# Weighted values of a head group: four key chunks in one TensorE burst instead of two bursts of two

## The reference

```python
# attention (x: 4 x 512 x 256, ctx: 4 x 512 x 256)
Q, K, V = heads(layernorm(x), Wq, bq), heads(ctx, Wk, bk), heads(ctx, Wv, bv)
scores = einsum('bhqd,bhkd->bhqk', Q, K) / sqrt(D) + adj
scores = where(mask == 0, -inf, scores)
out = einsum('bhqk,bhkd->bhqd', softmax(scores), V)     # the weighted values
x = x + tanh(g_xattn) * (out @ Wo.T + bo)
# experts (8, hidden 1024), one expert for each token by argmax of a softmax gate
x = x + tanh(g_ffn) * (relu(xn @ w1[e] + b1[e]) @ w2[e] + b2[e]) * gate_weight     # xn = layernorm(x)
```

## Time and profile before

| | us |
|---|---|
| median of 3 runs (lowest, highest) | 622.31 (622.23, 623.06) |
| profiled execution, its own time | 623.12 |
| its span | 621.3 |
| attention steps within the span | about 43 to 394 |
| PE busy in the span | 528.8 (85%) |
| DVE, ACT, POOL busy | 297.5, 303.9, 308.1 |
| line 821 on PE, 1024 records | 70.9 |

### The profile page before, as it was taken

The page is one execution under the profiler, slowest core; times in us unless marked ns, Lnnn a source line. Parts: engine busy times, 40 slices in busy tenths (PEclk is TensorE's granted clock), DMA queues, the critical chain, the costliest instruction groups (busy, mean ns, idle before and its releaser), DMA issues.

```text
span 621.3 us, 13413 instructions
## 1 busy us (share of the span) xinstructions
PE 528.8 (85%) x4008; PEld 401.0 (65%) x4009; DVE 297.5 (48%) x883; ACT 303.9 (49%) x674; POOL 308.1 (50%) x475
## 2 busy tenths in 40 slices
PE   4579999899999899999899988510989999999992
PEld 3247566566666566666566665310989999998882
DVE  2656677776678775678566876340011111111110
ACT  3536676556685556686566755200333333333320
POOL 6443485763584663584655537122344445445341
PEclk9879999999999899999899998955899999999997
DMA  8664139612149520149400181855455655555630
GB/s 294 213 215 138 64 103 210 136 68 70 40 139 198 102 69 2 60 133 194 92 2 2 51 271 45 288 108 138 113 184 181 204 191 205 195 190 185 186 93 1
DMA packets 62649, 83.43 MB, mean 134 GB/s; under 512 B 8920, under 2 KB 52008, under 8 KB 62472
## 3 DMA queue, kind: packets, MB, share of 16 engines
q1 hardware_dynamic: 58504, 74.53, 43.2%
q0 software_dynamic: 4096, 8.29, 4.6%
HBM read 69.54 MB, written 14.18 MB: 135 GB/s over the span
## 4 chain that ended last, share of the span: by engine, by line
PE 24%; DMA 16%; issue 9%; POOL 6%; DVE 5%; ACT 2%; POOLq 1%; DVEq 0%; SPq 0%; ACTq 0%
DMA out_y<-cT,sidx 13%; PE bank L809 6%; PE bank L821 5%; PE bank L799 3%; POOL rows L623 3%; PE bank L906 2%; PE bank L896 2%; DVE prob L1218 2%; DMA slot_d<-pair,posi 2%; PE bank L702 1%; ACT pt L986 1%; PE bank L783 1%; PE bank L737 1%; DMA rows<-xn_d,gidx 1%; PE bank L764 1%
## 5 line engine op out<-in xcount | busy, mean ns | idle before, releaser
L1218 DVE CUSTOM_DVE_ANT_0 prob<-bank,adjm 128x512 f32<-128x512 f32 x256 | 172.7, 688 | 95.5 <-issue 63.0
L571 POOL TENSOR_SCALAR prob<-prob,negmax 128x512 f32<-128x512 f32 x192 | 134.3, 704 | 143.4 <-DVE negmax L1218 135.4
L986 ACT ACTIVATE pt<-bank 128x512 f32<-128x512 f32 x256 | 150.9, 595 | 100.1 <-PE bank L809 94.4
L809 PE MATMUL bank<-ident,prob 128*128 128x128 f32 x1024 | 156.7, 276 | 7.3 <-POOL prob L571 3.4
L809 PEld LDWEIGHTS bank<-ident,prob 128*128 128x128 f32 x1024 | 126.7, 142 | 47.0 <-POOL prob L571 13.4
L1051 ACT ACTIVATE adjm<-bank,colsm 128x128 f32<-128x128 f32 x184 | 52.6, 368 | 113.9 <-PE bank L896 113.9
L799 PE MATMUL bank<-w2s 128*128 128x512 bf16 x256 | 99.4, 390 | 6.2 <-DMA w2s<-part_d 5.5
L1337 DVE TENSOR_TENSOR cT<-bank,maski 128x256 f32<-128x256 f32 x23 | 9.8, 424 | 172.1 <-PE bank L906 172.1
L896 PEld LDWEIGHTS bank<-xT,pt 128*128 128x128 f32 x736 | 88.3, 197 | 2.2 <-ACT xT L1042 1.0
L896 PE MATMUL bank<-xT,pt 128*128 128x128 f32 x736 | 88.6, 280 | 0.6 <-ACT xT L1042 0.6
L906 PE MATMUL bank<-w2s,adjm 128*128 x368 | 83.4, 380 | 0.0
(11 more groups left out here) (141 smaller groups left out, 502.3 us busy)
## 6 DMA issues: line engine op xcount, KB each, us to landing
pt<-in_L_ffn_w SPq DMA_DIRECT2D x23, 1024.0 KB
w2s<-part_d SPq DMA_DIRECT2D x48, 256.0 KB
w2s<-in_L_ffn_w SPq DMA_DIRECT2D x8, 1024.0 KB, 10.6
part_d<-parts SPq DMA_DIRECT2D x16, 384.0 KB, 2.6
maski<-in_mask_Bx1xSxS_ik SPq DMA_DIRECT2D x4, 1024.0 KB, 6.2
w2s<-part_d SPq DMA_DIRECT2D x32, 128.0 KB, 3.0
xres<-in_x SPq DMA_DIRECT2D x18, 128.0 KB
x_d<-rows SPq DMA_DIRECT2D x18, 128.0 KB, 2.5
```

The costliest lines, as they stand in the source:

```text
L571: po.tensor_scalar(prob[:, m], prob[:, m], -1.0, negmax[:, m:m + 1], ALU.mult, ALU.add).then_inc(s_shpool, 1)
L809: mm = pe.transpose(tr_bank[n % NTB][:, c * P:(c + 1) * P], prob[:, n % TILES % NB, c * P:(c + 1) * P], ident[:])
L986: act.activation(pt[:, g % 2, :, j, q2 * P:(q2 + 1) * P], tr_bank[c % NTB][:].rearrange("p (c q) -> p c q", c=QT), ACT.Exp).then_inc(s_cac ...
L1218: ve.tensor_tensor_reduce(out=prob[:, m % NB], in0=sc_bank[m % NS][:], in1=adjm[:, qt], scale=-1.0, scalar=BIG, op0=ALU.add, op1=ALU.min, ...
```

## The change

The test that picks the steps now picks every eighth step alone, and all four chunks run there, in step 13 + 8g. Step 15 + 8g has no weighted values any more. Nothing else changes: the same matmuls, the same semaphores, the same work on DVE, ACT, POOL and SyncE. The wait ahead of chunk 0 stays where it was, and the count that tells ACT that the group is done (`s_pv`) is given two steps earlier in the order.

```diff
-                if n >= LP + TPG and (n - LP) % TPG in (0, 2):
-                    g, c = divmod(n - LP - TPG, TPG)
-                    if g == 0 and c == 0:
+                if n >= LP + TPG and (n - LP) % TPG == 0:
+                    g = (n - LP - TPG) // TPG
+                    if g == 0:
                         pe.wait_ge(s_v, b * 2 + 2)
-                    weigh(b, g, c)
-                    weigh(b, g, c + 1)
+                    for c in range(QT):
+                        weigh(b, g, c)
```

## The result

| | before, same series | after |
|---|---|---|
| median (lowest to highest), 20 executions each, us | 623.59 (620.31 to 629.65) | 632.1 (625.88 to 636.22) |
| ratio, 95% interval | | 1.0132 (1.0106 to 1.0159) |
| profiled execution, own time and span, us | 623.12, 621.3 | 633.5, 631.7 |

The forecast was 624.6 with 620.3 to 627.5. The sign is right, the size is not: +8.2 us (6.6 to 9.9) against +2.3.

What follows compares the result with a forecast made beforehand. PE's order was taken to set the pace in the attention steps, PE being busy 85% of the span. Group gains and losses of +0.8 us plus +1.5 for clock falls gave +2.3, a median of 624.6 us, range 620.3 to 627.5.

Steps and rivals of the forecast that it cites:

- What joining saves: Each of 31 joins of two bursts saves 0.24 us of switching on PE, 7.4 us if PE waited for nobody.
- Steps 37 and 45 in batches 0 to 2, and 45 in batch 3: Joins there lose: +0.37 us through ACT's chain to `gate`, +0.86 through DVE's chain to `rank`.
- Batch 3: Last batch, where ACT has no next-batch work: groups of 13 to 37 gain 0.24 us each; whole batch -0.19.
- Group of step 61: `gate` of step 65 hangs on transposes of 64, behind both old bursts, so the join gains: -0.24 us.
- the group of 69: Both bursts lie inside POOL's `rstd` chain in batches 0 and 1: 0; batch 2 has no such work: -0.24 us.
- The cover term: Gains and losses of all groups over four batches sum to +0.8 us, bounds -0.7 to +2.8.
- The clock term: Emptier wait before `rank` drops PE's clock at two of four places: +1.5 us (0 to 6).
- the halving: A clock fall costs 1.5 us, but part ends in step 60's waits, so half was taken.
- the count: The clock was expected to fall at `rank` in two of the four batches.
- the prediction's own sign of being wrong: Wrong if `rank` waits no longer, the clock behind it stays 1.00, or step 60's waits change over 1 us.
- Rival 4: Clock falls at all four ranks and step 60 of batch 0, each for its full 1.5 us: 630.6; chance 0.06.
- Rivals 1 to 3: Clock holds: 623.1 us, chance 0.24; ACT gets ahead, only `rank` loses: 619.3, 0.13; all PE-bound: 614.9, 0.04.

Runs made afterwards that it cites:

- c3: Kernel before with only the bursts of steps 37 and 39 joined, in step 37; executed once, 625.74 us, read by steps alone.
- a2: Kernel before with only the bursts of steps 45 and 47 joined, in step 45; 628.73 us, 1.0093 of before.
- c2: Kernel before with only the bursts of steps 61 and 63 joined, in step 61; executed once, 628.26 us, read by steps alone.
- d1: Changed kernel plus 16 identity transposes ahead of the `rank` wait and 10 ahead of step 60's `normed` wait; 621.26 us, 0.9948 of before.
- a4: Changed kernel plus 16 identity transposes ahead of the `rank` wait; 625.35 us, 1.0032 of before.
- b2: Kernel before plus 11 identity transposes ahead of step 60's `normed` wait; 621.05 us, 1.0019 of before.
- c4: Kernel before with only the bursts of steps 45 and 47 joined, late, in step 47; 623.38 us, 1.0019 of before.
- a1: Changed kernel with every group's four chunks in step 15 + 8g in place of 13 + 8g; 623.01 us, 1.0003 of before.
- b3: Kernel before with groups of 13, 21, 29 joined early, those of 37 and 45 joined late in 39 and 47; 619.18 us, 0.9965 of before.
- a3: Changed kernel with the group of steps 45 and 47 left as two bursts; 625.39 us, 1.0037 of before.
- d2: b3 plus 8 identity transposes ahead of step 60's `normed` wait; 614.80 us, 0.9832 of before.

## Why the prediction was wrong in size

**What joining saves: right.** A long burst is 1.93 and the steps of the first three groups gain 0.22 to 0.33 each against 0.24, in every batch but the last's third (+0.30).

**Steps 37 and 45 in batches 0 to 2, and 45 in batch 3: right.** +0.37 and +0.86 forecast, +0.37 and +0.86 to +0.89 measured, by the chains that were named (ACT's to `x2T`, DVE's to `onehot`). `c3` and `a2` do each by itself and show the same step. That DVE never waits for PE in its chain is not quite what the trace shows: it puts 0.33 of idling ahead of two of its masks down to PE, but the same 0.33 before and after. The 0.6 of waiting ahead of `gate` is there, in small pieces at the transposes of steps 41 to 43, and not as idling of `gate` itself, which is 0.31 where it was 0.32.

**Batch 3: wrong, and the largest piece of the missed cover.** Forecast were gains of 0.24 for each of the groups of 13 to 37, -0.96. Measured: -0.20 and +0.39, together +0.19, so 1.15 us missed in one batch. "PE has other work" in these steps holds only where there is a next batch; in batch 3 PE comes up against ACT and POOL at once. That ACT has no work for a next batch there helps the group of 37 when it is joined alone (`c3`, -0.17) and not behind the other joins.

**Group of step 61: wrong.** "Behind both old bursts: -0.24" looked only at `gate`. DVE's mask stands one step behind the scores, and PE comes up against it once nothing lies between; +0.24 in batch 0 and `c2`'s +0.28 to +0.37 (-0.02 in batch 1 of the kernel after). In batch 2 the group of 69 didn't gain either (+0.20 for -0.24).

**The cover term (what moving costs, less what joining saves): too small.** Forecast +0.8 (bounds -0.7 to +2.8). The profiles at full clock give +2.8 (339.2 - 336.4), `d1` +2.6; the median less its clock 8.2 - 4.5 = 3.7, and `d1`'s median less its clock only +0.7. By the steps it lies at the upper bound, and the pieces that were too small are batch 3 and the groups of 61 and 69.

**The clock term: mis-sized, and the larger miss.** Forecast +1.5: two falls at 0.75. In the profile it is two falls at `rank` at about 1.2 and one doubled fall at step 60 with 1.4, 3.8 in these steps, less a fall that batch 3 has before and not after: 17.1 - 10.3 = 6.8 us more slow time, x 0.40 = 2.7 net. Over 20 executions it is 11.6 us more, 4.5. Two steps of the working failed. One is the halving: the time lost behind `rank` is not waited out in step 60, since DVE's chain there starts late too, and nearly the whole 1.5 comes through (1.2 to 1.3). The other is the count: two falls in four at `rank` was right, in this profile, but only `rank` was asked, and the fall at step 60 of batch 2 doubled. So the prediction's own sign of being wrong came up: the wait for `rows` in step 60 grew by 1.3 in batches 0 and 3. By profile, cover and clock make 2.8 + 2.7 = 5.5, which is what the attention steps grew by; by the slow time of 20 executions they make 2.8 + 4.5 = 7.3 of the measured 8.2, and 0.9 is left.

**The rivals.** Rival 4 (falls at every `rank`, 630.6) was nearest in time and wrong in place: `rank` fell in two batches of four, at full price only there. Rivals 1 to 3 are out: the clock did not hold, ACT was no help ahead of `gate`, and PE alone does not set the time.

**What stays open.** How the 8.2 divides: the cover is 2.6 to 2.8 by profiles, but `d1` against its own series leaves only +0.7, and the 3.7 of the medians is merely what the clock's 4.5 leaves of the 8.2. The clock is shown by `a4` against after, where nothing else moved up to `rank`; its price per us is a fit (0.39) in medians, while `a4` gave back 9.7 us of slow time and about 6 us of time. How often each place falls over many executions wasn't measured: only one profile of each kernel shows places.

## What to carry to other kernels

Joining small bursts saves the switch between them (0.24 us here), but the burst that is moved also takes cover away where it stood: place the long one behind the start of a latency chain on another engine (step 47, not 45: 0.2% against 0.9% slower), and not ahead of it. An emptied wait costs twice, once as idling and again as slower matmuls behind it, so the clock belongs in the sum of every edit that lengthens a wait, on both sides of the comparison. Cheap matmuls into a free bank ahead of such a wait gave back 1.0% in one kernel here, 0.4% in another (`a2`), and nothing in the kernel before (`b2`).

## What was not expected of the hardware

Of 16 profiles, 6 have a stall of 2.4 to 4.5 us around step 64 of batch 1, where PE's scores wait for the next batch's stacked operands; the kernels before and after have none in their profiles. Windows of `c4` through it:

```profile
204.00:208.00 4.00, 2.62 (x27) 1.60 (x27) 3.65 (x14) 2.04 (x4) 3.42 (x7) 1.00 1.50 190
208.00:212.00 4.00, 3.27 (x36) 2.07 (x32) 2.28 (x8) 1.73 (x4) 2.84 (x5) 1.00 0.65 28
212.00:216.00 4.00, 1.18 (x5) 1.04 (x6) 0.00 (x0) 0.00 (x0) 0.00 (x0) 0.74 0.51 45
```

and of `a1`, a different order of PE's work:

```profile
208.00:212.00 4.00, 1.72 (x30) 0.82 (x21) 0.37 (x3) 0.54 (x2) 0.93 (x2) 1.00 1.23 24
```

The same window of the kernel before, which has no such wait:

```profile
208.00:212.00 4.00, 4.00 (x30) 2.16 (x28) 2.08 (x9) 1.09 (x3) 3.45 (x6) 0.62 0.39 65
```

The rate drops in all of them at this place, before's too (158 GB/s in 204 to 208, then 65), so the drop alone isn't the stall. What differs is the share of time in which the DMA engines hold packets while little arrives: 0.65 at 28 GB/s and 1.23 at 24, against 0.39 at 65. It stands at the same place in kernels whose bursts differ, `b2` among them, which has the bursts of the kernel before; what causes it wasn't tried. In 4 of the 6 the clock fell around it too. Whether such stalls are part of why the kernel before itself ranges over 617.3 to 629.7 us, and of why `a1`, `b2`, `b3` and `c4` show less in their medians than in their steps, isn't shown; these four and `a3` and `d2` are the ones whose profile has one.
